# Squared norms of q and k: fp32 products of 32 stationary columns in place of bfloat16 halves, in a gated linear attention and mixture-of-experts kernel

## The reference

```python
def _l2norm(u, eps=1e-12):
    n = jnp.sqrt(jnp.sum(u * u, axis=-1, keepdims=True))
    return u / jnp.maximum(n, eps)
q = _l2norm((x @ Wq).reshape(Bb, Tt, H, DK))
k = _l2norm((x @ Wk).reshape(Bb, Tt, H, DK))
v = (x @ Wv).reshape(Bb, Tt, H, DV)
alpha = jax.nn.sigmoid(x @ Wg).reshape(Bb, Tt, H, DK)
def step(S, qkva):
    q_t, k_t, v_t, a_t = qkva
    S = a_t[..., None] * S + k_t[..., None] * v_t[:, :, None, :]
    o_t = jnp.einsum('bhkv,bhk->bhv', S, q_t)
    return (S, o_t)
```

## Time and profile before

| | |
|---|---|
| median of 3 runs | 2142.69 us (2139.69 to 2145.41) |
| the profiled execution, span from first to last instruction | 2138.3 us |
| TensorE busy | 2005.2 us, 94% |
| TensorE weight loads | 1690.3 us, 79% |
| VectorE busy | 1712.6 us, 80% |
| ScalarE busy | 1095.9 us, 51% |
| GpSimd busy | 922.1 us, 43% |
| mean granted clock of TensorE | 0.988 |

### The profile page before, as it was taken

One profiled execution on the slowest core, in us unless ns is written; L12 is line 12 of the kernel. 1 busy time (PEld: TensorE's weight loads), 2 busy tenths in 40 slices (PEclk: granted clock), 3 DMA queues, 4 the chain that ended last, 5 costly groups with the idle time before them and its releaser, 6 DMA issues.

```text
span 2138.3 us, 49851 instructions
## 1 busy us (share of the span) xinstructions
PE 2005.2 (94%) x16903; PEld 1690.3 (79%) x16903; DVE 1712.6 (80%) x3516; ACT 1095.9 (51%) x2352; POOL 922.1 (43%) x729
## 2 busy tenths in 40 slices
PE   7999999999999999999999999999988999999997
PEld 5888888888888888888888888888875666666664
DVE  4988888788878787888788787878885777777876
ACT  5555445455445455545455444555534555555554
POOL 5444444344434344444434444434422444444443
PEclk8999999999999999999999999999999999999999
DMA  6000000000000000000000000000000000000000
GB/s 182 2 6 7 2 6 2 7 1 7 1 7 2 7 6 2 6 2 7 2 7 2 7 1 7 2 7 6 2 1 11 21 10 20 20 10 20 20 10 15
DMA packets 28482, 24.53 MB, mean 11 GB/s; under 512 B 1928, under 2 KB 23696, under 8 KB 28304
## 3 DMA queue, kind: packets, MB, share of 16 engines
q1 hardware_dynamic: 28304, 21.77, 3.3%
HBM read 13.38 MB, written 4.19 MB: 8 GB/s over the span
## 4 chain that ended last, share of the span: by engine, by line
PE 51%; issue 21%; DVE 17%; POOL 9%; ACT 1%; DVEq 1%; POOLq 0%; DMA 0%; SPq 0%; ACTq 0%
PE bank L599 15%; DVE k_sb L1211 7%; PE bank L589 6%; PE bank L517 4%; POOL wq_lo L485 4%; PE bank L519 4%; PE bank L518 4%; POOL wk_lo L485 4%; PE bank L606 4%; PE bank L634 3%; PE bank L577 3%; PE bank L648 2%; PE bank L622 2%; DVE at_sb L1224 2%; DVE qq_sb L1172 2%
## 5 line engine op out<-in xcount | busy, mean ns | idle before, releaser
L441 POOL TENSOR_TENSOR sq_lo<-sq_sb,sq_hi 128x512 bf16<-128x512 f32 x256 | 348.7, 1362 | 581.0 <-ACT sq_hi L947 581.0
L1211 DVE TENSOR_TENSOR qq_sb<-qq_sb,tot_sb 128x512 f32<-128x512 f32 (+1 forms) x384 | 304.2, 792 | 195.6 <-PE bank L599 187.0
L599 PE MATMUL bank<-qq_sb,k_sb 128*128 128x64 f32 x3072 | 376.9, 276 | 12.9 <-DVE k_sb L1211 10.1
L599 PEld LDWEIGHTS bank<-qq_sb,k_sb 128*128 128x128 f32 x3072 | 364.8, 193 | 27.0 <-DVE k_sb L1211 16.3
L1211 DVE TENSOR_TENSOR k_sb<-k_sb,tot_sb 128x512 f32<-128x512 f32 (+1 forms) x384 | 298.6, 778 | 1.3 <-PE bank L606 1.3
L446 POOL TENSOR_TENSOR rn_sb<-ss_sb,expo 128x8 f32<-128x8 f32 x128 | 213.9, 1671 | 194.3 <-DVE ss_sb L1258 194.0
L1224 DVE COPY_PREDICATED at_sb<-mask_half,bank 128x512 f32<-128x512 int32 (+1 forms) x320 | 220.3, 730 | 0.0
L969 ACT ACTIVATE v_sb<-bank,rn_sb 128x128 f32<-128x128 f32 x512 | 139.0, 383 | 118.5 <-PE bank L519 107.8
L485 POOL TENSOR_TENSOR wq_lo<-v_sb,wq_hi 128x512 fp32r<-128x512 f32 x80 | 103.8, 1298 | 146.5 <-ACT wq_hi L1107 146.5
L485 POOL TENSOR_TENSOR wk_lo<-v_sb,wk_hi 128x512 fp32r<-128x512 f32 x80 | 104.3, 1304 | 133.3 <-ACT wk_hi L1107 133.3
L991 ACT ACTIVATE at_sb<-bank 32x256 f32<-32x256 f32 x64 | 23.8, 373 | 262.1 <-PE bank L606 262.1
(11 more groups left out here) (199 smaller groups left out, 4885.4 us busy)
## 6 DMA issues: line engine op xcount, KB each, us to landing
x_nat<-in_L_attn_x_dram SPq DMA_DIRECT2D x16, 256.0 KB, 2.7
x_nat<-x_all SPq DMA_DIRECT2D x16, 256.0 KB, 2.3
out_dram<-k_sb SPq DMA_DIRECT2D x16, 256.0 KB, 2.3
ew_raw<-in_L_ffn_exp_w_dram SPq DMA_DIRECT2D x3, 512.0 KB, 5.6
qq_sb<-in_L_attn_Wq_dram SPq DMA_DIRECT2D x1, 512.0 KB, 4.7
qq_sb<-in_L_attn_Wk_dram SPq DMA_DIRECT2D x1, 512.0 KB, 5.8
k_sb<-in_L_attn_Wg_dram SPq DMA_DIRECT2D x1, 512.0 KB, 6.6
k_sb<-in_L_attn_Wv_dram SPq DMA_DIRECT2D x1, 512.0 KB
```

The lines of the kernel that those rows point to most:

```text
L441: nc.gpsimd.tensor_tensor(sq_lo[:, n, :], sq_sb[:, n % 2, :], sq_hi[:, n, :], ALU.subtract).then_inc(sq_done, 1)
L599: mm = nc.tensor.matmul(bank[:, g * 64:(g + 1) * 64], k_sb[par][:, lo:lo + C], halves(qd_sb[par][:, lo:lo + C], HALF[j])[:, :, 1, :], star ...
L1211: return nc.vector.tensor_tensor(view, view, by, ALU.mult)
```

## The change

The squares of all four tiles are kept in fp32 (sq_sb now has four buffers); sq_hi, sq_lo, their square on ScalarE and the subtraction on GpSimd are gone. In sums_of_squares the ones are now the stationary operand, 32 columns wide, and the squares the moving one with 512 columns in fp32, one product per head. Each of the four tiles has its own 32 partitions of the result, and the sums lie along the free axis there. ScalarE copies them out of the bank into ss_row (take_sums), and TensorE turns them into the partitions with four small products against the identity (stand_sums: one fp32 matmul, three transposes). clamp_sums reads them with another stride, and clamp_sums(P + 1, 0) stands behind level 4 in place of level 3. sums_of_squares(P + 1, 1) now stands ahead of outputs_of_state.

```diff
@@ sums_of_squares on TensorE
-                pe.wait_ge(sq_done, P * 4 + (i + 1) * HP)
+                pe.wait_ge(sq_full, P * 4 + (i + 1) * HP)
...
                 for h in range(HP):
-                    for c in range(NC):
-                        col = (h * NC + c) * SS
-                        for part, sq in enumerate((sq_hi, sq_lo)):
-                            mm = nc.tensor.matmul((nb_ps, su_ps)[i][:, col:col + SS], sq[:, i * HP + h, c * C:(c + 1) * C],
-                                                  ones[:, :], start=part == 0, stop=part == 1)
+                    rows = slice((i * HP + h) * QD, (i * HP + h + 1) * QD)
+                    mm = nc.tensor.matmul((nb_ps, su_ps)[i][rows, :], ones_wide[:, 0:QD], sq_sb[:, i * HP + h, :], start=True, stop=True)
+                mm.then_inc(sr_full, 1)
+
+            def stand_sums(P, i):
+
+                pe.wait_ge(sr_evac, P * 2 + i + 1)
+                rows = slice(i * HP * QD, (i + 1) * HP * QD)
+                for c in range(NC):
+                    standing = (nb_ps, su_ps)[i][:, c * HP * QD:(c + 1) * HP * QD]
+                    lying = ss_row[rows, c * C:(c + 1) * C]
+                    if c == 0:
+                        nc.tensor.matmul(standing, lying, ident[rows, rows], start=True, stop=True)
+                    else:
+                        mm = nc.tensor.transpose(standing, lying, ident[rows, rows])
                 mm.then_inc(ss_full, 1)
@@ the slot on TensorE
                     if has_prev:
                         outputs_of_chunk(prev_p, P - 1, b if p else b - 1, 0)
                     if has_next:
+                        stand_sums(P + 1, 0)
                         project(next_p, P + 1, wg, 4)
                         project(next_p, P + 1, wg, 5)
                     scores(par, P, 5)
+                    if has_next:
+                        sums_of_squares(P + 1, 1, n_x)
                     if has_prev:
                         outputs_of_state(prev_p, P - 1, 0)
                     if has_next:
-                        sums_of_squares(P + 1, 1, n_x)
+                        stand_sums(P + 1, 1)
                         spread_norms(1 - par, P + 1)
@@ ScalarE
-                await_count(act, sq_done, P * 4 + n - 1)
-                nc.scalar.activation(sq_sb[:, n % 2, :], src, ACT.Square).then_inc(sq_full, 1)
-                nc.scalar.activation(sq_hi[:, n, :], src, ACT.Square).then_inc(sq_top, 1)
+                nc.scalar.activation(sq_sb[:, n, :], src, ACT.Square).then_inc(sq_full, 1)
+
+            def take_sums(P, i):
+
+                act.wait_ge(sr_full, P * 2 + i + 1)
                 await_count(act, ss_full, P * 2)
+                rows = slice(i * HP * QD, (i + 1) * HP * QD)
+                nc.scalar.activation(ss_row[rows, :], (nb_ps, su_ps)[i][rows, :], ACT.Copy).then_inc(sr_evac, 1)
...
                         square(1 - par, P + 1, 3)
+                        take_sums(P + 1, 0)
                         take_gate(1 - par, P + 1)
+                        take_sums(P + 1, 1)
@@ GpSimd
-                def low_square(n):
-                    pool.wait_ge(sq_full, P * 4 + n + 1)
-                    pool.wait_ge(sq_top, P * 4 + n + 1)
-                    nc.gpsimd.tensor_tensor(sq_lo[:, n, :], sq_sb[:, n % 2, :], sq_hi[:, n, :], ALU.subtract).then_inc(sq_done, 1)
...
-                for n in range(2 * HP - 1):
-                    low_square(n)
                 inverse_norms(0)
-                low_square(2 * HP - 1)
@@ VectorE
-                        if j == 3 and has_next:
+                        if j == 4 and has_next:
                             clamp_sums(P + 1, 0)
```

More of the change, by code:

```diff
@@ L77, in gated_linear_attention_and_moe_block @@
     STEPS = 8
-    SS = 32
+    QD = 32
     HALF = {j: 2 ** (j - 1) for j in range(2, STEPS)}
@@ L107, in gated_linear_attention_and_moe_block @@
         ident = sb("ident", [128, 128])
-        ones = sb("ones", [128, SS], bf16)
         ones_wide = sb("ones_wide", [128, 128])
@@ L130, in gated_linear_attention_and_moe_block @@
         v_sb = [sb(f"v_sb{i}", [128, NC, HP * D]) for i in range(2)]
-        sq_sb = sb("sq_sb", [128, 2, T])
-        sq_hi = sb("sq_hi", [128, 2 * HP, T], bf16)
-        sq_lo = sb("sq_lo", [128, 2 * HP, T], bf16)
+        sq_sb = sb("sq_sb", [128, 2 * HP, T])
+        ss_row = sb("ss_row", [128, T])
         kt_sb = sb("kt_sb", [128, HP, NC - 1, 128])
@@ L213, in gated_linear_attention_and_moe_block @@
         sq_full = sem("sq_full")
-        sq_top = sem("sq_top")
         pj_full = sem("pj_full")
@@ L218, in gated_linear_attention_and_moe_block @@
         xt_evac = sem("xt_evac")
-        sq_done = sem("sq_done")
+        sr_full = sem("sr_full")
+        sr_evac = sem("sr_evac")
         ss_full = sem("ss_full")
@@ L402, in pool_setup @@
                                     base=0, pattern=[[-1, 128]], channel_multiplier=1).then_inc(ident_done, 1)
-            nc.gpsimd.memset(ones[:, :], 1.0).then_inc(const_pool, 1)
             nc.gpsimd.memset(ones_wide[:, :], 1.0).then_inc(const_pool, 1)
@@ L409, in pool_setup @@
             nc.gpsimd.memset(spread[:, :, :], 0.0).then_inc(const_pool, 1)
-            pool.wait_ge(const_pool, 7)
+            pool.wait_ge(const_pool, 6)
             nc.gpsimd.affine_select(out=earlier[:, :, :], in_=earlier[:, :, :], compare_op=ALU.is_ge, fill=0.0,
@@ L420, in pool_setup @@
             for i in range(PARTS):
-                pool.wait_ge(const_pool, 12 + i)
+                pool.wait_ge(const_pool, 11 + i)
                 nc.gpsimd.affine_select(out=spread[:, :, :], in_=spread[:, :, :], compare_op=ALU.not_equal, fill=1.0,
@@ L427, in pool_setup @@
                                         base=m - 1, pattern=[[2 * m, 64 // m], [0, m]], channel_multiplier=-1).then_inc(const_pool, 1)
-        CONST_POOL = 19
+        CONST_POOL = 18
         @block.gpsimd
@@ L692, in _ @@
             sums_of_squares(0, 0, 1)
+            stand_sums(0, 0)
             pe.wait_ge(fold_sb, 4)
@@ L711, in _ @@
             sums_of_squares(0, 1, 1)
+            stand_sums(0, 1)
             spread_norms(0, 0)
@@ L942, in square @@
                 act.wait_ge(pj_evac, P * 8 + n + 1)
+                await_count(act, sr_full, P * 2)
+                src = (q_sb, k_sb)[n // HP][par][:, (n % HP) * T:(n % HP + 1) * T]
+                nc.scalar.activation(sq_sb[:, n, :], src, ACT.Square).then_inc(sq_full, 1)
+            def take_sums(P, i):
+                act.wait_ge(sr_full, P * 2 + i + 1)
                 await_count(act, ss_full, P * 2)
-                await_count(act, sq_done, P * 4 + n - 1)
-                src = (q_sb, k_sb)[n // HP][par][:, (n % HP) * T:(n % HP + 1) * T]
-                nc.scalar.activation(sq_sb[:, n % 2, :], src, ACT.Square).then_inc(sq_full, 1)
-                nc.scalar.activation(sq_hi[:, n, :], src, ACT.Square).then_inc(sq_top, 1)
+                rows = slice(i * HP * QD, (i + 1) * HP * QD)
+                nc.scalar.activation(ss_row[rows, :], (nb_ps, su_ps)[i][rows, :], ACT.Copy).then_inc(sr_evac, 1)
             def take_gate(par, P):
@@ L1016, in _ @@
             nc.scalar.activation(gate_t[:, 0:E], sc[0][:, 2 * D:2 * D + E], ACT.Copy).then_inc(fold_sb, 1)
+            take_sums(0, 0)
             for n in range(2):
@@ L1021, in _ @@
             nc.scalar.activation(swf[0][:, :], sc[0][:, :], ACT.Copy).then_inc(w_hi, 1)
+            take_sums(0, 1)
             take_gate(0, 0)
@@ L1257, in clamp_sums @@
                 await_count(dve, rn_done, (P - 1) * 2 + i + 1)
-                nc.vector.tensor_scalar(ss_sb[:, i * G:(i + 1) * G], (nb_ps, su_ps)[i][:, 0:G * SS:SS], L2_EPS * L2_EPS, None,
+                nc.vector.tensor_scalar(ss_sb[:, i * G:(i + 1) * G].rearrange("p (h c) -> p h c", h=HP), (nb_ps, su_ps)[i][:, 0:G * QD].rearrange("p (c h x) -> p h c x", h=HP, x=QD)[:, :, :, 0], L2_EPS * L2_EPS, None,
                                         ALU.max).then_inc(ss_evac, 1)
```

1 line of the change is left out of this document (removed).

## The result

The changed kernel takes 2245.56 us (median of 4 runs, 2244.82 to 2247.68) where the kernel before took 2141.19 us (4 runs): 1.0488 times as long, 95% interval 1.0472 to 1.0505. It is slower by 104 us, inside the predicted range, 77 us under the predicted time and less than 3 us above the range's lower end.

A forecast was written before the change was run, and what follows sets the result against it. TensorE was taken as the bound: per slot +3.6 us of work and waiting less 0.8 us recovered, net +2.8 us, over 63 slots +177 us, plus 3 us at the start, on 2142.7 us: 2323 us, range 2243 to 2390 us.

The forecast's parts named there:

- TensorE is the bound: In the attention loop TensorE sets the slot, with about 1.0 us per slot of waits other than the back edge.
- The sums: sums_of_squares on TensorE: two fp32 products per group at 1.54 us, 3.1 us per slot, replacing 0.8 us of bfloat16 products.
- the changes of shape: On TensorE, each change of tile shape between neighbouring groups costs 0.1 us.
- its own signs: Wrong if first sums take a microsecond or less, slots grow no more than a microsecond, or TensorE waits longer for VectorE.
- three halves: In sums_of_squares, the two products overlap by one record each, 1.44 us a group; chance 0.5.
- the full overlap: Rival for sums_of_squares: both products run side by side, 0.96 us a group, 2263 us in all; chance 0.2.
- The turn: stand_sums on TensorE: one fp32 product, three transposes and a shape change, 0.57 us each, 1.15 per slot.
- What it gets back: TensorE's waits before lines 606 and 599 go: 0.8 of 1.0 us per slot recovered, the back edge stays.
- GpSimd: Four subtractions of 1362 ns per slot go from GpSimd; worth nothing to 0.3 us per slot, taken as nothing.
- The faster case: Rival: VectorE's path rules; without line 441 its multiplies shorten and TensorE's waits go, 2088 us; chance 0.04.
- the later clamp: clamp_sums(0) at level 4 delays GpSimd's first power by about 4 us; hidden, since spread_norms is itself 2 us later.
- the start: In slot 0 TensorE waits for both copies and runs two dearer groups: +3 us.

The follow-up runs named there:

- e2: The kernel before without GpSimd's four subtractions per slot, TensorE multiplying the high halves twice: 2086.81 us, ratio 0.9743.
- e1: The changed kernel with both fp32 products of a group writing the same 32 partitions, so the same column group: 2358.90 us.
- e5: The changed kernel with the second group of sums moved back behind outputs_of_state, directly ahead of its stand_sums: 2294.04 us.
- e4: The changed kernel without take_sums and stand_sums, the clamp reading the bank as it lies: 2170.42 us.
- e3: The changed kernel with four GpSimd subtractions per slot put back as extra work that nobody on the path waits for: 2249.83 us.
- e8: The kernel before with the subtractions kept, but TensorE waiting only for ScalarE's bfloat16 squares and multiplying the high halves twice: 2141.77 us.
- e7: The kernel before with bfloat16 squares alone, without low halves, their subtraction and the fp32 squares: 2081.61 us, ratio 0.9720.
- e10: The kernel before with fp32r squares as stationary operand against 32 columns of ones, no halves, subtraction or turn: 2134.60 us, ratio 0.9967.

## Why the prediction was right in sign and too high

**TensorE is the bound: right.** The pure work of the quiet slot was put at 22.87 us from one hole in the timeline; e2 shows 22.84. After the change the slot with the layer norm and the quiet one are level at 25.68, and e1 and e5 show that what is added to TensorE is paid in full.

**Luck in the range.** The sum was 3.6 us of added work and 0.8 us of waits recovered, and measured are 2.84 and 1.24 us, as worked out below. The sums were put 1.1 us too dear and a wait of 0.15 us didn't come, but the changes of shape were put 0.6 us too cheap and offset part of it. Without that offset, some 38 us, the time would have been below the range. By its own signs the prediction failed on three points: it called itself wrong "if the first group of sums takes a microsecond or less", and the group takes 0.98 us; the slots were to take about 27.5 us and take 25.68; and the short wait for ss_row isn't there.

**The sums: right in kind, mis-sized.** "I take the overlap to be between the second record of the first and the first record of the second: three halves, 1.44 us." It is 0.98 us, shape included, the full overlap that I gave 0.2, and e1 shows that the column groups do it. With 0.1 us for the shape I had 3.1 us for two groups; they take 1.96. This is the largest of the wrong terms, 1.1 us per slot or some 70 us. The rule of the Trainium skill ("TensorE: Matmul & The Clock Gate", Part 3) that tiles in different column groups run concurrently held. I had drawn my three halves from its rule that matmuls start and end in program order, and from an assumption that I didn't check, that both records of the first product come before those of the second. The records start in pairs 7 ns apart, so the first record of each product runs beside that of the other, which the rule doesn't forbid. The records of line 606, my own row for the overlap, stand in such pairs in the trace before: the first four start at 887.119, 887.125, 887.171 and 887.178 us.

**The turn: right.** 0.55 us each was 0.57 in the sum. The changes of shape were under-counted: TensorE's work per slot rose by 25.68 - 22.84 = 2.84 us, of which 1.96 - 0.81 = 1.15 are sums and 1.10 the turn. The other 0.6 lies in the groups around them: 0.15 us in outputs_of_state, some 0.17 in the outputs of the chunk, 0.1 in scores(5) and the rest ahead of and behind the sums. I had 0.4 for four changes, all told, and had it inside the terms for the sums and the turn. "TensorE stands still for about 0.15 us" before the second stand_sums would fit the 0.15 us by which outputs_of_state grew, but it isn't that wait: the copy is over 0.16 us before the turn, where e5 needs 0.06. The group ahead of the first stand_sums grows too, where ScalarE is done 2 us before. e4 has 0.77 us for outputs_of_state, so 0.05 us came with its place behind the sums and 0.10 with the turn behind it. That it is the change of shape which costs this is an inference: each such group stands next to one of another shape.

**What it gets back: too low.** Waits per slot, back edge and transposes of x included, were 24.65 - 22.84 = 1.81 us and are 26.25 - 25.68 = 0.57. 1.24 us came back where I counted 0.8, 28 us in 63 slots. 63 x (2.84 - 1.24) = 101 us, against my 177.

**GpSimd: wrong.** "From nothing to 0.3 us per slot; I take nothing, since TensorE's longer work covers it." The second half holds (e3: 4 us), the first doesn't: taken alone it is worth 0.9 us per slot (e2, e8). The step that failed is the search for multiplies beside line 441 itself. One such stands before scores(5) in the slot with the layer norm, whose wait was in my rows, so "GpSimd is on that path in none of these places by line 441" was false for it. And between scores(5) and scores(7), where I was right that no subtraction lies, the subtraction still acts by way of VectorE's small product and GpSimd's block product (e2): the multiply at 885.33 takes its 1.13 us beside the block product, on the path and not beside line 441. By these sums the waits that came back in the changed kernel, 1.24 us, are for the greater part waits that GpSimd had caused, 0.9 us. The faster case that I gave 0.04 named this mechanism and priced it at 63 x 0.86 us; e2 finds 56 us. It didn't decide because the fp32 products and their turn cost 2.8 us per slot. The agreement is partly luck: it counted on one or two multiplies that fall from 1.22 to 0.68 us, read at level 3, and the waits that went stood before scores(5) and scores(7). That the relief and TensorE's longer work would both take away the same waits, so that they don't add up, is what e2 and e3 together show.

**ScalarE, the later clamp, the start: right.** No wait for ss_row is left in the quiet slot, the chain doesn't touch VectorE between scores(5) and scores(7), and the start cost 3.8 us for 3.

## What to carry to other kernels

Before work is moved from a half-idle engine to the one that bounds the kernel, ask what each of the two is worth by itself: here GpSimd's silence was worth 56 us and TensorE's new work, 2.84 us in each of 63 slots, some 180 us. The variant with the first and without the second beats both kernels: e7 by 2.8% against the kernel before, at the price of bfloat16 rounding, and e10, where the squares are rounded to fp32r instead, by 0.3%. A busy share of 43% doesn't show what an engine costs its neighbour; the neighbour's mean duration by form does, and a run without the traffic prices it. An instruction can cost time at a place where it doesn't run, by shifting another one, so a search along the path for its direct neighbours isn't enough. Once the bounding engine covers a wait, whatever else would have removed it is worth little: 4 us here in place of 56.

## What the runs showed of the hardware

- Two fp32 products with 512 moving columns and 32 stationary ones take 0.98 us together in two column groups and 1.83 us in the same group; in two groups their records start in pairs, 7 ns apart.
- An fp32 product with 128 stationary and 32 moving columns takes 0.21 us (two records of 0.106), one in fp32r 0.10 to 0.11 us, one in bfloat16 0.025 us.
- GpSimd's tensor_tensor on 128x512 stretches VectorE's beside it: a product of 128x128 from 281 to 643 ns in the mean, one of 128x64 from 214 to 496 ns. The power on 128x8, 1.67 us at 880.34, doesn't: VectorE's multiply beside it at 881.27 takes 0.69 us.
- A group ahead of one with another shape of tile takes about 0.1 to 0.17 us more than ahead of one with its own; that the shape is the cause is inferred.
